# Causal attention between two stages of a transformer layer: a third score bank, and the end of each query block written out in place

## The reference, cut to what matters

```python
scores = jnp.einsum('bqhd,bkhd->bhqk', q, k) * scale
causal = jnp.tril(jnp.ones((T, T), bool))
scores = jnp.where(causal, scores, jnp.finfo(scores.dtype).min)
probs = jax.nn.softmax(scores, axis=-1)
attn = jnp.einsum('bhqk,bkhd->bqhd', probs, v)
```

## Time and profile before

| | |
|---|---|
| timed executions | 12,306.79 and 12,466.24 us, median 12,386.51 us |
| profiled execution | 12,396.39 us, span of its slowest core (2) 12,394.9 us |
| spans of the eight cores | 12,283.4 to 12,394.9 us |
| granted TensorE clock, mean of each core | 0.670 to 0.676 |
| busy share over the span of core 2 | PE 53%, DVE 45%, ACT 13%, POOL 7% |
| attention stage on core 2 | about 2,488 to 5,783 us; granted clock 0.62 |

### The profile page before, as it was taken

The page is one execution under the profiler, slowest core; times in us unless marked ns, Lnnn a source line. Parts: engine busy times, 40 slices in busy tenths (PEclk is TensorE's granted clock), DMA queues, the critical chain, the costliest instruction groups (busy, mean ns, idle before and its releaser), DMA issues. The chain is left out here.

```text
span 12394.9 us, 57055 instructions; the slowest of 8 cores (12283.4 to 12394.9 us)
## 1 busy us (share of the span) xinstructions
PE 6600.3 (53%) x20055; PEld 2084.2 (17%) x20459; DVE 5541.2 (45%) x8746; ACT 1650.5 (13%) x2649; POOL 837.6 (7%) x704
## 2 busy tenths in 40 slices
PE   3473554577777878786232235777776023040505
PEld 1131211111111111111010012323332001020202
DVE  4524445422222232322424424333334977959594
ACT  0000000022222222221101101000000111111110
POOL 1000000000000000000212211111110000000000
PEclk8786767756666666666565566877887556575757
DMA  3124222200000000001141121111111023050504
GB/s 85 48 70 107 75 64 82 83 14 25 14 25 14 20 18 18 21 13 30 34 61 40 36 45 25 36 36 36 36 36 35 10 45 73 9 107 12 104 15 94
DMA packets 291576, 542.87 MB, mean 44 GB/s; under 512 B 91420, under 2 KB 190937, under 8 KB 270809
## 3 DMA queue, kind: packets, MB, share of 16 engines
q0 software_dynamic: 32192, 198.19, 9.1%
q1 hardware_dynamic: 245017, 311.64, 8.4%
q10 hardware_dynamic: 14080, 29.37, 0.9%
HBM read 617.74 MB, written 119.54 MB: 59 GB/s over the span
## 5 line engine op out<-in xcount | busy, mean ns | idle before, releaser
L1622 PE MATMUL o_ps<-iqT,w_sb 128*128 128x512 bf16 x2759 | 707.4, 406 | 2100.0 <-DVE iqT L1589 2041.5
L1268 PE MATMUL f_ps<-xqT,w_sb 128*128 128x512 bf16 x2756 | 783.0, 444 | 620.3 <-DMA w_sb<-w3w 615.2
L836 ACT ACTIVATE probs<-sc_ps,negc_bc 128x512 bf16<-128x512 f32 x1280 | 880.1, 688 | 1719.9 <-PE sc_ps L830 1719.9
L844 DVE TENSOR_TENSOR probs<-probs,mask_sb 128x512 bf16<-128x512 bf16 x512 | 217.9, 426 | 1932.5 <-ACT probs L836 1932.5
L971 PE MATMUL o_ps<-at_sb,ow_sb 128*128 128x512 bf16 x1000 | 367.6, 543 | 849.8 <-DMA ow_sb<-ow 829.1
L1622 PEld LDWEIGHTS o_ps<-iqT,w_sb 128*128 128x128 bf16 x2816 | 280.6, 101 | 2527.8 <-DVE iqT L1589 2077.6
L1280 PE MATMUL f_ps<-xqT,w_sb 128*128 128x512 bf16 x2759 | 697.0, 407 | 4.0
L1544 DVE TENSOR_TENSOR mb<-mb,cb 128x512 f32<-128x512 f32 x1056 | 678.9, 684 | 0.0
L830 PE MATMUL sc_ps<-qTr,kTr 64*128 64x512 bf16 x1280 | 653.2, 510 | 38.6 <-issue 38.1
L854 PE MATMUL av_ps<-probs,vh 128*128 128x512 bf16 x1258 | 641.5, 510 | 28.1 <-DVE probs L844 28.1
L863 PE MATMUL r_ps<-probs,ones_st 128*1 128x512 bf16 x1280 | 627.9, 491 | 7.7 <-issue 6.9
(11 more groups left out here) (266 smaller groups left out, 7940.5 us busy)
## 6 DMA issues: line engine op xcount, KB each, us to landing
w_sb<-w2w POOLq DMA_DIRECT2D x64, 1408.0 KB, 11.0
xnb_t<-x_nat SPq DMA_DIRECT2D x32, 1024.0 KB, 7.2
xtb_c<-xT SPq DMA_DIRECT2D x128, 256.0 KB, 2.9
ow_sb<-ow POOLq DMA_DIRECT2D x64, 512.0 KB, 6.2
w_sb<-w1w POOLq DMA_DIRECT2D x44, 512.0 KB, 5.7
w_sb<-w3w POOLq DMA_DIRECT2D x44, 512.0 KB, 7.5
gw_s<-gw_t SPq DMA_DIRECT2D x176, 128.0 KB, 1.8
gw_c<-gw_s SPq DMA_DIRECT2D x176, 128.0 KB, 2.4
```

Of the source, the lines that this page charges most:

```text
L836: ex = p.op("s", lambda e, bank=bank, slot=slot: e.activation(probs[slot][:], sc_ps[bank][:], AF.Exp, bias=negc_bc[:], scale=1.0), deps=[m ...
L1268: e.matmul(f_ps[p1b][:], w1_sb[wpar][:, dc * 128:(dc + 1) * 128], xqT[:, dc * MYT + blk * 512: dc * MYT + (blk + 1) * 512], start=(dc == 0 ...
L1622: stop = p.op("t", lambda e, kc=kc, wp=wp, bk=bk: e.matmul(o5_ps[bk][:], w2_sb[wp][:, kc * 128:(kc + 1) * 128], iqT[:, kc * 512:(kc + 1) * ...
```

## The change

It does two things. The scores rotate over three PSUM banks (`ci % 3`) where they had two. And `emit_qtail`, `pend_tail` and `st_qt` are gone: the tail stands at the end of its own block, ahead of the next block's shift broadcast. The matmul that broadcasts the reciprocal now names the shift copy as what it waits for, and the next block's shift broadcast waits for the copy out of bc_ps. The buffer of the values is given back after the last values matmul (`av_stop`) and not after the astage product.

```diff
-            sc_ps = [e2(nc.psum_tensor(f"sc_ps{i}", [128, 512], F32)) for i in range(2)]
+            sc_ps = [e2(nc.psum_tensor(f"sc_ps{i}", [128, 512], F32)) for i in range(3)]
...
-            pend_tail = None
-
-            def emit_qtail(tq_, qc_, h_, avs_, rs_):
-                rr = p.op("v", lambda e: e.tensor_copy(rrow[:], r_ps[:]), deps=[rs_])
...
                     bq = p.op("t", lambda e, Qi=Qi: e.matmul(
                         bc_ps[:, 0:1], ones_bc[:], ncg[0:1, Qi:Qi + 1],
                         start=True, stop=True, skip_group_check=True),
-                        deps=[ngc, st_qt["bc_war"]])
+                        deps=[ngc, bc_war])
                     ncg_war = bq
                     nbc = p.op("v", lambda e: e.tensor_copy(negc_bc[:], bc_ps[:, 0:1]),
                                deps=[bq, negc_war])
-                    st_qt["bc_war"] = nbc
-                    if pend_tail is not None:
-                        tq_, qc_, h_, avs_, rs_ = pend_tail
-                        emit_qtail(tq_, qc_, h_, avs_, rs_)
-                        pend_tail = None
+                    bc_war = nbc
...
-                        bank = ci & 1
+                        bank = ci % 3
...
-                    pend_tail = (Qi, qc0, h, av_stop, r_stop)
+                    rr = p.op("v", lambda e: e.tensor_copy(rrow[:], r_ps[:]),
+                              deps=[r_stop])
+                    r_war = rr
+                    ri = p.op("v", lambda e: e.reciprocal(rinv[:], rrow[:]), deps=[rr])
+                    bq2 = p.op("t", lambda e: e.matmul(
+                        bc_ps[:], ones_bc[:], rinv[:], start=True, stop=True,
+                        skip_group_check=True), deps=[ri, nbc])
+                    rbc = p.op("v", lambda e: e.tensor_copy(rinv_bc[:], bc_ps[:]),
+                               deps=[bq2, av_war])
+                    bc_war = rbc
+                    apar = Qi & 1
+                    ast = p.op("v", lambda e, apar=apar: e.tensor_tensor(
+                        astage[apar][:], av_ps[:], rinv_bc[:], ALU.mult),
+                        deps=[av_stop, rbc, ast_war[apar]])
+                    av_war = ast
...
-                tq_, qc_, h_, avs_, rs_ = pend_tail
-                emit_qtail(tq_, qc_, h_, avs_, rs_)
-                pend_tail = None
-                buf_war[par] = [sc_war[0], sc_war[1], st_qt["av_war"], mm1, mm2]
+                buf_war[par] = [sc_war[0], sc_war[1], av_stop, mm1, mm2]
```

More of the change, by code:

```diff
@@ L717, in build_nc @@
             probs_war = [None] * 4
-            sc_war = [None, None]
-            st_qt = {"av_war": None, "r_war": None, "bc_war": None}
+            sc_war = [None, None, None]
+            av_war = None
+            r_war = None
+            bc_war = None
             ast_war = [None, None]
-            pend_tail = None
-            def emit_qtail(tq_, qc_, h_, avs_, rs_):
-                rr = p.op("v", lambda e: e.tensor_copy(rrow[:], r_ps[:]), deps=[rs_])
[L725 to L741, removed]
             for h in range(NH):
@@ L851, in build_nc @@
                         if cj == 0:
-                            avd.append(st_qt["av_war"])
+                            avd.append(av_war)
                         av_stop = p.op("t", lambda e, cj=cj, slot=slot_j, par=par, n=ncch:
@@ L860, in build_nc @@
                         if cj == 0:
-                            rd.append(st_qt["r_war"])
+                            rd.append(r_war)
                         r_stop = p.op("t", lambda e, cj=cj, slot=slot_j, n=ncch:
@@ L868, in build_nc @@
                         pend_av = (ci, slot, ptok)
-                    pend_tail = (Qi, qc0, h, av_stop, r_stop)
+                    rr = p.op("v", lambda e: e.tensor_copy(rrow[:], r_ps[:]),
[13 more added lines that the diff above has]
+                    av_war = ast
+                    ast_war[apar] = p.dma("q", f"ast{apar}",
+                                          attnT_s.ap()[h * 128:(h + 1) * 128,
+                                                       qc0:qc0 + 512],
+                                          astage[apar][:], deps=[ast])
                     negc_war = ex
-                tq_, qc_, h_, avs_, rs_ = pend_tail
-                emit_qtail(tq_, qc_, h_, avs_, rs_)
-                pend_tail = None
-                buf_war[par] = [sc_war[0], sc_war[1], st_qt["av_war"], mm1, mm2]
+                buf_war[par] = [sc_war[0], sc_war[1], av_stop, mm1, mm2]
             p.barrier()
```

## The result

| | before | after |
|---|---|---|
| timed executions | 10, median 12,325.7 us (12,226.8 to 12,523.3) | 11, median 12,529.4 us (12,472.8 to 12,703.3) |
| ratio to before | | 1.0184, 95% interval 1.0144 to 1.0225 |
| profiled execution, slowest core | span 12,394.9 us | span 12,491.1 us |
| attention stage, mean of eight cores | 3,281 us | 3,490 us |
| fast blocks of 8, 16, 24, 32 chunks, of 128 each | 18, 98, 31, 117 | 20, 40, 96, 32 |

A forecast was written before the change was run, and what follows sets the result against it. PE inside a block, the chain at each block boundary and the clock a block gets were taken to set the attention stage. 12,396.4 + 0 + 43 + 92 = 12,531 us, forecast as 12,525 us, range 12,420 to 12,665.

The forecast's parts named there:

- the forecast's case: Attention stage: the clock is dealt out anew and nearly evenly among the blocks, 12,525 us; chance 0.59.
- Third bank, 0 us: Score matmuls (L823): a third score bank only removes waits for an exp; 0.0 us of matmul idle, so 0 us.
- Boundaries, +0.98 and +0.77 us, +43 us: Between query blocks, after a fast and a slow block: the score load comes later, 48 boundaries x 0.9 us.
- The shift copy hidden, head ends and SP as they were: DVE's 0.16 us shift copy ends before the first score matmuls do; order at head ends and on SP stays.
- The clock, +92 us: Attention stage: longer boundaries change which blocks reach full clock; +3.8 + 19.2 - 53.2 + 122.5 = +92 us.
- fast blocks of about 2, 10, 7 and 9 out of 16: Predicted blocks of 8, 16, 24 and 32 chunks reaching full clock; 3, 13, 3, 14 on core 2 before.
- my row prices: Saving per fast block of 8, 16, 24, 32 chunks, from profiled block windows: 3.8, 6.4, 13.3, 24.5 us.
- The replay: Repeats each core's block sequence, clock course set by block start times; gave 3,400 to 3,430 us with the longer boundaries.
- The rival of the boundaries alone: Only boundary lengths count and the pattern of fast blocks stays: 12,396 + 43 = 12,439 us; chance 0.15.
- The rival of a slower kernel by over 2%: The longest blocks lose the clock, 32 chunks fast 4 times of 16: +288 us, 12,684 us; chance 0.16.
- The signs that I had named: New trace: shift broadcast waits 48 times, stage 3,400 to 3,430 us, clock about 0.60; wrong if other stages move over 30 us.

The follow-up runs named there:

- the kernel before and 0.07 us: Kernel before, order and two banks untouched, plus a 128x224 scratch copy on DVE at each inner boundary: ratio to before 1.0140, stage 3,446 us.

## Why the prediction was right

It said 12,525 us (12,420 to 12,665) from an execution of 12,396 us, +1.0%. The measured median is 12,529 us, but that nearness is luck in part: the median of before turned out 60 us below the two runs that I had. As a ratio I forecast 1.010 and 1.0184 was measured. The direction, the range and both mechanisms hold; one term was too small, and the chip did not deal out the clock as evenly as the forecast's case had it.

- *Third bank, 0 us.* Right: 1.0007 by itself, and 0.0 us of idle ahead of the score matmuls.
- *Boundaries, +0.98 and +0.77 us, +43 us.* Right: +0.99 and +0.79 us by the medians. With the new shares of fast and slow blocks, 48 boundaries per core took 339.4 us before (147 of 384 at 6.82, the rest at 7.23) and 380.7 us after (156 at 7.81, the rest at 8.01), +41 us.
- *The shift copy hidden, head ends and SP as they were.* Right, by the timeline above; the time from a head's last r load to the next head's first score load stayed at 45.54 us (medians, after a fast block).
- *The clock, +92 us.* The right mechanism, too small. The stage grew by 209 us, so the term measured is 209 - 41 = +168 us. The step that was mis-sized is "fast blocks of about 2, 10, 7 and 9 out of 16": measured 2.5, 5, 12 and 4. Summed over the blocks of each length, that came to +3 us (8 chunks), +48 (16), -105 (24) and +220 (32) per core, 166 us in all. At my row prices those counts would give +198 us: I had taken the price of a 32-chunk block, 24.5 us, from one that became fast early, while before's 117 fast ones took 46.9 us on average, 21.2 us less than a slow one. The replay's warning fits, that 0.01 to 0.02 us more per boundary lead to about +230 us in all; the boundaries measured 0.01 to 0.015 us above my sum. What puts the executions on that side is not settled. Slow blocks lasted 0.002 to 0.003 us longer than before, with two banks as with three. The replay also read its border off before's blocks alone, and by my comparison 24 blocks of the changed kernel became fast where it had them slow; none of the rows shown here lists them, so take that as argued.
- *The rival of the boundaries alone* falls, with the kernel before and 0.07 us. *The rival of a slower kernel by over 2%* was near: the longest blocks did lose the clock, 4 of 16 as priced there, but the blocks of 24 chunks won it 12 times instead of 4 and paid nearly half back (105 of 220 us). The interval's upper end, 1.0225, reaches into it.
- *The signs that I had named* came out in part. The new wait stands 48 times, 0.06 us after the copy, and the boundaries are within 0.02 us. But the stage is 3,490 us and not 3,400 to 3,430, its clock on core 2 is 0.56 and not 0.60, and the blocks of 32 and 24 chunks are fast 4 and 12 times and not 9 and 7. And other stages moved by more than the 30 us that I had called a sign of being wrong: 57 and 56 us shorter, where no instruction differs. The change does not explain that, and the feed-forward part goes both ways from kernel to kernel (2,029 to 2,121 us); this is why the stage is judged by itself.

The Trainium skill's rule that the ramp penalty is under 1% of a typical kernel span and need not be fitted ("TensorE: Matmul & The Clock Gate", section "What's actually happening") does not hold for this kernel, if one leaves the clock term out by it: that term measured 168 us, 1.4% of the kernel. The single block of 24.5 us with which I argued was no proof of it, and my own 92 us would have been 0.7%, within the rule. The experiments are the proof: two kernels differ by the size of a scratch copy, 0.23 us at 48 boundaries or 11 us in all, and their attention stages by 3,676 - 3,205 = 471 us, 3.8% of the kernel. The same page's section "Loop structure matters more than you think" says that the loop nest decides whether matmuls stay at full clock; there the trace agrees: the stage's granted clock rose from 0.62 to 0.76 once the stall was gone.

## What to carry to other kernels

Where PE stands still for some microseconds between blocks of matmuls, read the granted clock block by block before costing an edit: here nearly one microsecond more at each of 48 boundaries was worth 41 us by its length and 168 us by what the clock did. Such a term is a property of exact lengths, so a kernel tuned to it is tuned to an accident; a delay of 0.07 us was enough to lose it in one kernel's stage and to win it in the other's. The remedy is not a better length but no stall: move the dependent tail behind some chunks of the next block's matmuls.

## What the runs showed that I had not expected

- A tiny DVE copy put between a copy and the reciprocal that waits for it cost nothing (128x16, 0.15 us long), one of 0.25 us cost 0.07 us and one of 0.48 us cost 0.30 us: the first 0.18 us fit beside the hand-over of the first copy's result.
- The same work can have the full clock or lack it: in the earlier trace rows and above, 66.5 us of matmuls in 68.1 us ran at 0.50 from end to end, in the same program in which a block of the same work reached full speed early and took 43.53 us.
